# First self attention of a two-layer decoder: projections transposed, placed by transfers, scores as pairs of 64-row products

## The reference

```python
B, S, D, H = (4, 512, 256, 16)              # at run time x is (1, 2048, 256)
HD = D // H
b, s, d = x.shape
h, hd = (H, d // H)
xc = jnp.transpose(x, (0, 2, 1))[..., None]
xc = jax.lax.conv_general_dilated(xc, conv_w, window_strides=(1, 1), padding=((1, 1), (1, 1)), dimension_numbers=('NCHW', 'OIHW', 'NCHW'), feature_group_count=d)
xs = jnp.transpose(xc[..., 0], (0, 2, 1))
xs = xs + xs @ pe_w.T
qkv = (xs @ qkv_w.T).reshape(b, s, 3, d)
qkv = jnp.transpose(qkv, (0, 2, 1, 3))
q = qkv[:, 0].reshape(b, h, s, hd).astype(jnp.bfloat16)
k = qkv[:, 1].reshape(b, h, s, hd).astype(jnp.bfloat16)
v = qkv[:, 2].reshape(b, h, s, hd).astype(jnp.bfloat16)
scale = jnp.sqrt(jnp.asarray(hd, dtype=jnp.bfloat16))
scores = jnp.einsum('bhqd,bhkd->bhqk', q, k) / scale
attn = jax.nn.softmax(scores, axis=-1)
o = jnp.einsum('bhqk,bhkd->bhqd', attn, v)
```

## Time and profile before

| what | value |
|---|---|
| median of the runs shown (3) | 4719.99 us (4715.94 to 4722.8) |
| the profiled execution, its own time | 4709.82 us |
| its span, first to last instruction | 4708.1 us |
| mean granted clock of TensorE over the span | 0.787 |
| TensorE busy | 4004.5 us (85%) |
| VectorE busy | 2573.7 us (55%) |
| ScalarE busy | 1753.8 us (37%) |
| GpSimd busy | 1558.4 us (33%) |

### The profile page before, as it was taken

The page is one execution under the profiler, slowest core; times in us unless marked ns, Lnnn a source line. Parts: engine busy times, 40 slices in busy tenths (PEclk is TensorE's granted clock), DMA queues, the critical chain, the costliest instruction groups (busy, mean ns, idle before and its releaser), DMA issues. The chain is left out here.

```text
span 4708.1 us, 69377 instructions
## 1 busy us (share of the span) xinstructions
PE 4004.5 (85%) x23609; PEld 2148.7 (46%) x23609; DVE 2573.7 (55%) x5577; ACT 1753.8 (37%) x2220; POOL 1558.4 (33%) x985
## 2 busy tenths in 40 slices
PE   7999999999989999999997705758888888888458
PEld 4555555555545555545553504623454333333225
DVE  3766666666635566666663291023327757773352
ACT  3444444444424444444443101211023545554230
POOL 0444444444407778777787001200010000000000
PEclk9555555555579999999998757879897989997569
DMA  0000000000000000000001105510002102110000
GB/s 28 1 0 0 0 0 0 0 0 0 20 21 5 10 10 10 12 8 10 10 10 46 63 19 160 161 45 5 0 19 25 17 9 25 13 13 3 1 29 18
DMA packets 80265, 97.20 MB, mean 21 GB/s; under 512 B 24341, under 2 KB 64024, under 8 KB 78681
## 3 DMA queue, kind: packets, MB, share of 16 engines
q1 hardware_dynamic: 77018, 90.51, 7.5%
q0 software_dynamic: 3072, 4.34, 0.5%
HBM read 66.29 MB, written 16.93 MB: 18 GB/s over the span
## 5 line engine op out<-in xcount | busy, mean ns | idle before, releaser
L291 DVE TENSOR_SCALAR_CACHE_REDUCE rows<-pS 128x1024 bf16<-128x1024 f32 x512 | 626.9, 1225 | 344.5 <-PE pS L240 344.3
L352 POOL TENSOR_SCALAR rows<-rows,mn 128x1024 bf16<-128x1024 bf16 x512 | 566.2, 1118 | 696.5 <-DVE mn L301 696.5
L363 ACT ACTIVATE prT<-pP 128x1024 bf16<-128x1024 bf16 x512 | 523.9, 1024 | 633.8 <-PE pP L252 633.8
L1264 DVE TENSOR_REDUCE x0hm<-x0pM 128x1 f32<-128x400 f32 (+1 forms) x1024 | 523.7, 563 | 239.5 <-PE x0pM L1180 239.4
L1641 DVE TENSOR_REDUCE x1hm<-x1pM 128x1 f32<-128x400 f32 (+1 forms) x1024 | 513.3, 566 | 167.4 <-PE x1pM L1555 167.2
L252 PEld LDWEIGHTS pP<-ident_b,rows 128*128 128x128 bf16 x4096 | 392.3, 140 | 399.6 <-issue 258.5
L240 PE MATMUL pS<-kT,qT 16*128 (+1 forms) x1024 | 524.7, 613 | 51.7 <-issue 31.6
L1720 ACT ACTIVATE x1pr<-x1pST 128x1024 f32<-128x1024 f32 (+1 forms) x416 | 405.2, 1021 | 346.8 <-PE x1pST L1586 346.6
L252 PE MATMUL pP<-ident_b,rows 128*128 128x128 bf16 x4096 | 526.9, 310 | 0.6 <-ACT prT L363 0.5
L1149 POOL TENSOR_TENSOR x0acc<-x0acc,x0pr 128x1024 f32<-128x1024 f32 (+1 forms) x176 | 419.6, 2384 | 110.8 <-ACT x0pr L1351 93.0
L1149 POOL TENSOR_TENSOR x0acc<-x0acc,o_nat 128x1024 f32<-128x1024 f32 (+1 forms) x176 | 419.5, 2383 | 62.5 <-ACT o_nat L1351 42.3
(11 more groups left out here) (347 smaller groups left out, 5490.6 us busy)
## 6 DMA issues: line engine op xcount, KB each, us to landing
m_w<-in_moe_w1T SPq DMA_DIRECT2D x16, 1024.0 KB, 4.9
m_w<-in_moe_w2T SPq DMA_DIRECT2D x16, 1024.0 KB, 5.4
heads_d<-x0on SPq DMA_DIRECT2D x32, 256.0 KB, 2.5
x0ooT<-heads_d SPq DMA_DIRECT2D x4, 2048.0 KB, 16.9
x1sq<-x1qh SPq DMA_DIRECT2D x32, 128.0 KB, 4.5
x1sk<-x1kh SPq DMA_DIRECT2D x32, 100.1 KB, 3.6
rows_d<-m_xr SPq DMA_DIRECT2D x1, 2176.0 KB, 7.8
acc_d<-m_zero SPq DMA_DIRECT2D x1, 2056.0 KB, 9.1
```

The lines of the kernel that those rows point to most:

```text
L291: nc.vector.tensor_scalar(rows[u][:, half * 1024:(half + 1) * 1024], pS[half][:, :], 1.0, None, ALU.mult, ALU.max, accum_out=mx[u][:, half ...
L352: nc.gpsimd.tensor_scalar(r, r, mn[u][:, 0:1], 1.0, ALU.add, ALU.mult).then_inc(s_df, 1)
L363: nc.scalar.activation(prT[u][:, half * 8:(half + 1) * 8, :], pP[half][:, :, :], ACT.Exp, scale=1.0 / HD ** 0.5).then_inc(s_ex, 1)
L1264: emptied(nc.vector.tensor_reduce(hm[g % 2][:, a, t, i % 8 // 2:i % 8 // 2 + 1], bank(name)[:, 0:w], AX.X, ALU.max, negate=True), name)
```

## The change

- Queries and keys are projected transposed: features on the partitions, tokens along the columns, in units of 512 columns (`q_unit`, `k_unit`, L203 of the new program), values as before but alone (`v_unit`). ScalarE copies queries to `qp`, VectorE keys to `kp`; values are shared between the two. `pA` is four single banks, used in turn.
- The transposes of the second part are gone. `qT` is now 128 partitions by 16 groups by 2048 tokens, `kT` 128 partitions by 8 places by 2048. GpSimd clears both (two memsets). SyncE then moves the 16 features of each group with a transfer of its own: queries twice, to partitions 0-15 and 64-79, keys once, groups c % 8 < 4 to partitions 0-15 and the others to 64-79. That is 48 transfers for each 512 tokens, and 192 in all; TensorE waits for all of them (s_rows) in a block of its own ahead of the attention.
- A score product reads 64 rows (16 features and 48 zeros). The two products of a half take rows 0-63 and rows 64-127.
- TensorE's steps are all written out; the other engines keep their loop.
- The negation (L301) is gone. `mx` is bf16 and `mb` f32, the maximum of step n-1 stands between the two roundings of step n, and GpSimd subtracts `mb` (same length, same operands otherwise).

The diff, cut to its core:

```diff
-        qk = m.sb("qk", [P, NT, 2 * D], BF16)
+        qT = m.sb("qT", [P, 16, T], BF16)
+        kT = m.sb("kT", [P, 8, T], BF16)
...
+            qp = m1.sb("qp", [P, DJ, T], BF16)
+            kp = m1.sb("kp", [P, DJ, T], BF16)
+            pA = [m1.ps(f"pA{i}", [P, 512]) for i in range(4)]
...
+            def xs_unit(n, j):
+                return 2 * n + j
+
+            def q_unit(n, j):
+                return 8 + 4 * n + j
+
+            def k_unit(n, j):
+                return 8 + 4 * n + 2 + j
+
+            def v_unit(t):
+                return 24 + t
...
+                    sp.wait_ge(s_zero, 2)
+                    for n in range(4):
+                        cols = slice(n * 512, (n + 1) * 512)
+                        sp.wait_ge(s_q, 2 * n + 2)
+                        for c in range(16):
+                            mine = slice(16 * (c % 8), 16 * (c % 8) + 16)
+                            for a in range(2):
+                                sp.dma_start(qT[64 * a:64 * a + HD, c, cols], qp[mine, c // 8, cols]).then_inc(s_rows, 16)
+                        sp.wait_ge(s_k, 2 * n + 2)
+                        for c in range(16):
+                            mine = slice(16 * (c % 8), 16 * (c % 8) + 16)
+                            a, place = c % 8 // 4, 4 * (c // 8) + c % 4
+                            sp.dma_start(kT[64 * a:64 * a + HD, place, cols], kp[mine, c // 8, cols]).then_inc(s_rows, 16)
...
+                    nc.gpsimd.memset(qT[:, :, :].bitcast(F32), 0.0).then_inc(s_zero, 1)
+                    nc.gpsimd.memset(kT[:, :, :].bitcast(F32), 0.0).then_inc(s_zero, 1)
...
+                    for n in range(4):
+                        for j in range(DJ):
+                            dve.wait_ge(s_full, k_unit(n, j) + 1)
+                            nc.vector.tensor_copy(kp[:, j, n * 512:(n + 1) * 512],
+                                                  pA[k_unit(n, j) % 4][:, :]).then_inc(s_k, 1)
+                    for t in range(1, NT, 2):
+                        dve.wait_ge(s_full, v_unit(t) + 1)
+                        nc.vector.tensor_copy(v1[:, t, :, 0:HD],
+                                              pA[v_unit(t) % 4][:, 0:D].rearrange("p (c d) -> p c d", d=HD))\
+                            .then_inc(s_vd, 1)
...
+                    for n in range(4):
+                        pe_.wait_ge(s_xs, 2 * n + 2)
+                        for x in range(2):
+                            for j in range(DJ):
+                                i = k_unit(n, j) if x else q_unit(n, j)
+                                wait_emptied(pe_, i - 4)
+                                for k in range(DJ):
+                                    mm = nc.tensor.matmul(pA[i % 4][:, :],
+                                                          wqkv[:, k, x * D + j * P:x * D + (j + 1) * P],
+                                                          xs[:, k, n * 512:(n + 1) * 512], start=(k == 0), stop=(k == 1))
+                                mm.then_inc(s_full, 1)
...
-                    for i in range(2 * H):
-                        for b in range(2):
-                            if i >= 2:
-                                pe_.wait_ge(s_tc if b == 0 else s_kc, i - 1)
-                            for c in range(8):
-                                col = b * D + (i % 2) * 128 + 16 * c
-                                mm = nc.tensor.transpose(pT[b + 2 * (i % 2)][:, c * P:(c + 1) * P],
-                                                         qk[:, i // 2, col:col + 16], G.ident_b[:, :])
...
+                    pe_.wait_ge(s_rows, 4 * 48 * 16)
...
                         wait(pe_, s_rd, 2 * (n - 1) + half + 1, n - 1)
                         for a in range(2):
-                            mm = nc.tensor.matmul(
-                                pS[half][:, a * 512:(a + 1) * 512], qT[:, bass.ds(n * P, P)],
-                                kT[:, bass.ds((n // 16) * T + half * 1024 + a * 512, 512)],
-                                start=True, stop=True)
+                            rows_a = slice(64 * a, 64 * a + 64)
+                            mm = nc.tensor.matmul(pS[half][:, a * 512:(a + 1) * 512], qT[rows_a, n % 16, head(n)],
+                                                  kT[rows_a, 4 * half:4 * half + 4, head(n)], start=True, stop=True)
...
-                    run(pe_, step)
+                    for n in range(NS):
+                        step(n, n % NU)
...
-                        if not first:
-                            maximum(n - 1, (u - 1) % NU)
                         if outputs:
                             sums(n - 7, b)
                         rounded(n, u, 0)
                         if not first:
-                            negated(n - 1, (u - 1) % NU)
+                            maximum(n - 1, (u - 1) % NU)
                         if outputs:
                             recip(n - 7, b)
                         rounded(n, u, 1)
...
-                        pool.wait_ge(s_mc, n + 1)
+                        pool.wait_ge(s_mx, n + 1)
 
                         pool.sem_inc(s_go, 1)
                         for half in range(2):
                             r = rows[u][:, half * 1024:(half + 1) * 1024]
-                            nc.gpsimd.tensor_scalar(r, r, mn[u][:, 0:1], 1.0, ALU.add, ALU.mult).then_inc(s_df, 1)
+                            nc.gpsimd.tensor_scalar(r, r, mb[u][:, 0:1], 1.0, ALU.subtract, ALU.mult).then_inc(s_df, 1)
...
```

More of the change, by code:

```diff
@@ L148, in _ @@
                                                       xc[:, k, n * 512:(n + 1) * 512], start=(k == 0), stop=(k == 1))
-                            mm.then_inc(s_pe, 1)
-                    for t in range(NT):
-                        pe_.wait_ge(s_xs, min(8, 2 * (t // 4) + 2) if t < 12 else 8)
-                        if t < 2:
-                            pe_.wait_ge(s_xs, 8)
-                        else:
-                            pe_.wait_ge(s_cp, t - 1)
-                        for a, w in ((0, 512), (1, 256)):
-                            for k in range(DJ):
-                                mm = nc.tensor.matmul(pA[t % 2][:, a, 0:w], xs[:, k, t * P:(t + 1) * P],
-                                                      wqkv[:, k, a * 512:a * 512 + w], start=(k == 0), stop=(k == 1))
-                        mm.then_inc(s_mm, 1)
+                            mm.then_inc(s_full, 1)
@@ L162, in _ @@
+                    for t in range(NT):
+                        i = v_unit(t)
+                        wait_emptied(pe_, i - 4)
+                        for k in range(DJ):
+                            mm = nc.tensor.matmul(pA[i % 4][:, 0:D], xs[:, k, t * P:(t + 1) * P],
+                                                  wqkv[:, k, 2 * D:3 * D], start=(k == 0), stop=(k == 1))
+                        mm.then_inc(s_full, 1)
                 @block.scalar
                 def _(act):
-                    for t in range(NT):
-                        act.wait_ge(s_mm, t + 1)
-                        nc.scalar.activation(qk[:, t, :], pA[t % 2][:, 0, :], ACT.Copy)
-                        nc.scalar.activation(v1[:, t, :, 0:HD],
-                                             pA[t % 2][:, 1, 0:D].rearrange("p (c d) -> p c d", d=HD),
-                                             ACT.Copy).then_inc(s_cp, 1)
@@ L172, in l0_attention_heads @@
-        qT = m.sb("qT", [HD, H * T], BF16)
-        kT = m.sb("kT", [HD, H * T], BF16)
-        with ExitStack() as c1:
-            m1 = Mem(nc, c1, sems)
-            pT = [m1.ps(f"pT{i}", [HD, 1024], BF16) for i in range(4)]
-            s_tr, s_tc, s_kc = m.sem("c_tr"), m.sem("c_tc"), m.sem("c_kc")
+                    for n in range(4):
+                        for j in range(DJ):
+                            act.wait_ge(s_full, q_unit(n, j) + 1)
+                            nc.scalar.activation(qp[:, j, n * 512:(n + 1) * 512], pA[q_unit(n, j) % 4][:, :], ACT.Copy)\
+                                .then_inc(s_q, 1)
@@ L178, in l0_attention_heads @@
+                    for t in range(0, NT, 2):
+                        act.wait_ge(s_full, v_unit(t) + 1)
+                        nc.scalar.activation(v1[:, t, :, 0:HD],
+                                             pA[v_unit(t) % 4][:, 0:D].rearrange("p (c d) -> p c d", d=HD),
+                                             ACT.Copy).then_inc(s_va, 1)
             with nc.Block() as block:
@@ L210, in l0_attention_heads @@
             prT = [m2.sb(f"prT{i}", [P, 16, P], BF16) for i in range(NU)]
-            mx = [m2.sb(f"mx{i}", [P, 2]) for i in range(NU)]
-            mb = [m2.sb(f"mb{i}", [P, 1], BF16) for i in range(NU)]
-            mn = [m2.sb(f"mn{i}", [P, 1]) for i in range(NU)]
+            mx = [m2.sb(f"mx{i}", [P, 2], BF16) for i in range(NU)]
+            mb = [m2.sb(f"mb{i}", [P, 1]) for i in range(NU)]
             sb_ = [m2.sb(f"sums{i}", [P, 2], BF16) for i in range(2)]
@@ L235, in _, with head @@
                 def _(pe_):
```

(9 more changed lines are left out.)

50 lines of the change are left out of this document (22 added, 28 removed).

## The result

The changed kernel takes 5512.05 us (median of 4 runs, 5505.71 to 5513.09) against 4718.07 us (median of 4 runs, 4715.94 to 4722.8) before: 1.1678 times as long, 95% interval 1.1658 to 1.1699. It is 794 us slower. The prediction was 4300 us, with 0.94 for faster. The profiled execution has a span of 5511.4 us and a mean granted clock of 0.741.

The account below looks back on a forecast made before the run. The prediction took TensorE at half clock in the first attention to bound the kernel: 4709.8 - 475 (attention steps) + 62 (longer setup) = 4297, with the runs' offset 4300 us; range 4225 to 4440.

Parts of the forecast that it names:

- Part 3: First attention at full clock: which engine bounds the step; 2.62 us a step, 684 us for 1159, -475 us.
- the last rival: Slower: TensorE starves fetching written-out instructions; the step must stay below 4.28 us; at 4.8 the time is 4845; chance 0.04.
- What bounds the kernel: First attention: TensorE bounds it at half clock, 4.52 us a step in the loop, 4.27 written out.
- Part 1: Score products: pairs run side by side, a half drops from 0.97 to about 0.54 us, the step to 3.43.
- the rival with the low clock: First attention: the clock stays low, TensorE's step is 3.43 us, the time 4499, about 4505; chance 0.10.
- Part 2, the clock: First attention: filled pairs instead of narrow products let the clock rise from 0.50 to the high level for the whole stage.
- Part 3, the bound of a step: First attention at high clock: VectorE's own 2.5 us mostly hides in GpSimd's ring; step 2.62 us, bounds 2.45 to 2.85.
- the ring: VectorE and GpSimd in turn: maximum 0.16, release 0.21, GpSimd's two halves 2.21, then the next maximum: 2.58 us.
- Part 3, the shorter chain: VectorE to GpSimd: the chain of maxima loses one instruction, L301, since GpSimd subtracts instead of adding a negated maximum.
- Part 4: Way to the first attention: clears delay VectorE, 192 transfers on one queue; first score product at 182 instead of 120.1, +62 us.
- TensorE short of instructions: First attention, the last rival: some 80 written-out instructions a step must all be fetched; at 60 ns each 4845; chance 0.04.

Follow-up runs that it names:

- Experiment 1: The kernel before with only GpSimd's form changed: the maximum copied instead of negated, GpSimd subtracting instead of adding; 5459.02 us, ratio 1.1576.
- experiment 2: The changed kernel with the maximum taken and negated in one VectorE reduction and GpSimd adding it again; 4253.27 us, ratio 0.9017.
- experiment 5: The kernel before with TensorE's 256 steps written out and nothing else changed; 4661.53 us, ratio 0.9871.
- experiment 4: negmax_add with score products reading only the 16 real rows of each half, without the zero rows; 4510.68 us (one run).
- negmax_add: The kernel of experiment 2: the changed kernel with a negated maximum from one VectorE reduction and GpSimd adding it; 4253.27 us, ratio 0.9017.
- before_subtract: The kernel of Experiment 1: the kernel before with GpSimd subtracting a copied maximum instead of adding a negated one; 5459.02 us, ratio 1.1576.
- experiment 6: The changed kernel with its two-input maximum kept, GpSimd multiplying by -1.0 then adding it, and the exponential's scale negated; 4263.53 us, ratio 0.9034.
- experiment 7: negmax_add with the kernel before's two-instruction chain back: two-input maximum ahead of both reductions, negation between them; 4337.28 us, ratio 0.9212.
- few_late_clear: negmax_add with 48 transfers of 2048 columns instead of 192 of 512, and both clears started only after VectorE's convolution; 4177.53 us, ratio 0.8851.

## Why the prediction was wrong

**The step that failed** is in Part 3: "GpSimd subtracts instead of adding a negated maximum", costed as GpSimd's two halves of before, "2.21". Experiment 1 shows that this form takes 2 x 3.70 = 7.40 us (7.36 from step to step), so GpSimd bounds the step, and nothing else is needed for the loss. I took the price of an instruction with another operation from the row of the old one, and gave it no bound above. Neither the range nor a rival held it; no row of before shows that form. The nearest row that I passed over was GpSimd's additions of two tiles in the next stage, unchanged by the change (2386 ns in the kernel before); from the page of the changed kernel:

```profile
L1170 POOL TENSOR_TENSOR x0acc<-x0acc,x0pr 128x1024 f32<-128x1024 f32 (+1 forms) x176 | 419.6, 2384 | 111.0 <-ACT x0pr L1372 93.4
```

Two of these would have been 4.77 us a step, above the 4.28 at which the last rival put the even point. A bound worked out from that row would have opened the other side, though still far short of 7.36. Now the other steps, with experiment 2 as the change that I costed:

- *What bounds the kernel* (TensorE at the low clock): right. Written out, the step is 4.21 us (4.27 forecast), and the whole gain of that is 58 us (experiment 5).
- *Part 1, pairs side by side*: right. At the low clock the step of such pairs is 3.38 us (3.43 forecast; experiment 4), and the time 4510.68 us where the rival with the low clock said 4505.
- *Part 2, the clock*: right in negmax_add, 1.00 through the stretch, and its condition is shown by experiment 4: with the same order of work and only the zero rows taken out, it stays 0.50. The Trainium skill's rule ("TensorE: Matmul & The Clock Gate", Part 4: PE-mode transpose), that transposes don't count, had been taken to mean a low level here; negmax_add, half of whose columns on TensorE are transposes, runs at 1.00. The rule itself isn't borne out by the kernel before: from 90 to 118 us TensorE had nothing but transposes, and the clock stayed at 1.00 (most of that stretch is in the earlier trace rows). Experiment 4 doesn't speak on it, since both of its kernels have the same transposes. In the changed kernel itself the clock was 0.50, with TensorE busy for 145 us of 300. That this is for the long waits is argued, not tested; TensorE isn't the bound there, and before_subtract has the same pace of GpSimd with its old score products.
- *Part 3, the bound of a step*: the engine is VectorE and not the ring; the ring term was 0.15 us too long, since the maximum lies beside GpSimd's end (experiment 6). The maximum was forecast at about 0.5 us, as L297 before, and took 0.15. The step is 2.46 us against 2.62, 249 x 0.16 = 40 us less than the sum, and 4300 - 40 = 4260 is what negmax_add takes to within 7 us.
- *Part 3, the shorter chain*: worth more than the ring said, 84 us at the high clock (experiment 7). At the low clock TensorE, busy for 300 of 300 us in experiment 5 with the longer chain, hides it.
- *Part 4*: +62 forecast, +63 measured to the first score product. The pieces agree too: 0.62 us an issue forecast, 0.63 measured; landing 1.8, not 3.9. The Trainium skill's rule ("SBUF — State Buffer", Who interferes with whom), that a GpSimd instruction which only writes locks out VectorE's fast two-port operations alone, agrees with the trace: the two scalings wait for the clears (7.96 and 3.25 us against 1.29) and the four other instructions of the chain keep their 2.35. The wait goes both ways: the clear of `kT`, beside whose beginning the first scaling ran, took 8.00 us, and 6.92 in few_late_clear.
- *TensorE short of instructions*: didn't happen. In negmax_add its waits in the steps are for VectorE.

## What to carry to other kernels

An instruction whose operation changes is a new instruction: if no row of the trace has that form, its price is open on both sides, and an engine with half of its time free can become the bound by it. Measure the form alone, in place, before the rest of the change is judged; one edit here separated 794 us lost from 460 us gained. And where two engines wait for each other in turn, ask which instruction's input is already there when it comes: by experiment 7's trace, moving a small instruction behind the next long one was worth more (0.22 us a step) than leaving one out (0.06).

## What the runs showed of the hardware

- GpSimd's elementwise instruction with per-partition operand, 128x1024 bf16 in place: multiply with add in either order 1.11 to 1.12 us; add alone or subtract alone 2.84; add with add, add with the smaller-of, subtract with add, subtract with multiply in either order 3.70 to 3.71. Why is not shown. Whether multiplication alone is quick, and whether f32 values behave alike, wasn't tried.
- VectorE's two-input maximum of two values a partition waits for GpSimd's instruction, but not always to its end. In the kernel before, beside the quick form, 254 of 256 ended 1.12 to 1.13 us after the start of a GpSimd instruction, which is its end. In the changed kernel the instruction lasts 3.70 us, and the line of the maximum is

```profile
L325 DVE TENSOR_TENSOR mb<-mx x256: 153/154/1445, 187.5 to 2049.6; 128x1 f32<-128x1 bf16 x128
```

There, five that began early in a GpSimd instruction ended 1.12 us after its start; 250 began 1.66 us or more after that start, with 0.34 us or more of the instruction to go, and took 0.15 us. So here the slow forms held VectorE's two-input instruction for their first 1.12 us only.
- Rows of zeros in the array are not only free but useful: products of 16 real and 48 zero rows, in pairs, ran at a granted clock of 1.00, and the same pairs without the zeros at 0.50, 257 us apart in the whole time (4510.68 against 4253.27). At the low clock one such product takes 605 ns with the zero rows (the changed kernel) and 603 without. The added rows hold nothing but zeros, so no value in them lifts the clock. Whether lone products of 64 rows would do wasn't tried in this stage; at lone f32 ones of the next the clock fell (1396).
- SyncE's issues cost 0.63 us each, whether a transfer carries 16 or 64 KB.
